# Turning attention's output in 32x32 blocks on VectorE instead of by products on TensorE and transposing transfers

## What is computed

```python
qkv = x @ w_qkv                                   # 16 heads, q, k, v of 16 columns each
scores = einsum('...hqd,...hkd->...hqk', q, k) / sqrt(256)
attn = softmax(where(causal, scores, -1e30))
out = einsum('...hqk,...hkd->...qhd', attn, v).reshape(..., 256)
return out @ w_o
...
h = layernorm(x) * (1 + ca) + sa
x = x + ga * attention(h)
h = layernorm(x) * (1 + cb) + sb
x = x + gb * ffn(h)                               # shared silu(h w1) * (h w2) w3 + the two chosen experts
```

## Time and profile before

| | us |
|---|---|
| median of 3 runs | 1907.32 (1906.16 to 1908.15) |
| the profiled execution, its own time | 1906.43 |
| its span | 1904.7 |
| TensorE busy | 1759.5 (92%) |
| VectorE busy | 1506.3 (79%) |
| ScalarE busy | 1126.2 (59%) |
| GpSimd busy | 955.2 (50%) |

### The profile page before, as it was taken

How to read it: one execution, slowest core, us unless ns; L and a number is a source line. 1 busy time by engine, 2 the same in 40 slices (tenths; PEclk the granted TensorE clock), 3 DMA queues, 4 the chain that set the end, 5 groups by cost and what they waited for, 6 DMA issues and landing times. The chain is left out here.

```text
span 1904.7 us, 46834 instructions
## 1 busy us (share of the span) xinstructions
PE 1759.5 (92%) x17886; PEld 1014.6 (53%) x17886; DVE 1506.3 (79%) x2717; ACT 1126.2 (59%) x1486; POOL 955.2 (50%) x1015
## 2 busy tenths in 40 slices
PE   5677899999999999999999999999999999989987
PEld 2233435455554454445454545454545788778764
DVE  7886788887988787788878888988896486755777
ACT  2687867676767576767666766776676333222211
POOL 2444555365436553654454554545555267534423
PEclk8788999999999999999999999999999999999989
DMA  4243331223122312231122122221312777766997
GB/s 144 74 150 84 119 70 44 68 58 97 24 74 55 96 32 66 56 96 41 58 58 85 44 60 54 83 63 47 85 52 83 167 159 165 176 142 145 276 315 260
DMA packets 248840, 191.58 MB, mean 101 GB/s; under 512 B 181344, under 2 KB 216936, under 8 KB 246832
## 3 DMA queue, kind: packets, MB, share of 16 engines
q1 hardware_dynamic: 235472, 152.26, 32.1%
q0 software_dynamic: 12960, 36.06, 5.5%
q10 hardware_dynamic: 192, 0.26, 0.1%
HBM read 65.23 MB, written 62.19 MB: 67 GB/s over the span
## 5 line engine op out<-in xcount | busy, mean ns | idle before, releaser
L1176 ACT ACTIVATE arena<-pair 128x1024 f32<-128x1024 f32 (+1 forms) x640 | 575.5, 942 | 195.3 <-PE pair L1898 192.4
L1370 DVE TENSOR_REDUCE max_part<-pair 128x2 f32<-128x1024 f32 (+2 forms) x448 | 535.0, 1219 | 95.6 <-PE pair L1874 91.7
L1935 PE MATMUL pair<-feat_parts,ffn_sb 128*128 128x512 f16 x1536 | 379.0, 383 | 9.9 <-DMA feat_parts<-rows 5.4
L1920 PE MATMUL pair<-arena,v_sb 128*32 128x256 f32 (+1 forms) x5120 | 325.1, 367 | 2.0 <-ACT arena L1176 1.0
L950 POOL TENSOR_SCALAR_AFFINE_SELECT arena<-arena 128x512 f32<-128x512 f32 x256 | 169.5, 670 | 290.7 <-ACT arena L1176 290.4
L1874 PE MATMUL pair<-arena 48*128 48x128 f16 (+3 forms) x2304 | 209.9, 280 | 40.7 <-DMA arena<-parts 13.5
L1898 PE MATMUL pair<-arena 50*128 50x256 f16 (+1 forms) x2560 | 210.4, 264 | 22.6 <-DVE max_part L1370 7.9
L1935 PEld LDWEIGHTS pair<-feat_parts,ffn_sb 128*128 128x128 f16 x1536 | 132.7, 98 | 179.5 <-issue 38.6
L1959 PE MATMUL pair<-parts,arena 128*128 128x256 f16 x1704 | 209.6, 282 | 18.5 <-DMA parts<-lists 10.0
L1036 POOL DMA_INDIRECT slots<-arena,feat x142 | 145.0, 1021 | 145.9 <-DVE arena L1599 116.0
L1042 POOL TENSOR_TENSOR hidden<-silu_h,hidden 128x512 f16<-128x512 f32 x128 | 151.4, 1187 | 121.0 <-ACT hidden L1211 120.0
(11 more groups left out here) (221 smaller groups left out, 2251.5 us busy)
## 6 DMA issues: line engine op xcount, KB each, us to landing
arena<-parts SPq DMA_DIRECT2D x380, 64.0 KB, 2.3
rows<-x SPq DMA_DIRECT2D x8, 1024.0 KB, 5.4
x_sb<-x SPq DMA_DIRECT2D x16, 512.0 KB, 4.8
base<-norm SPq DMA_DIRECT2D x14, 512.0 KB, 3.2
ffn_parts<-hidden SPq DMA_DIRECT2D x8, 768.0 KB, 4.1
arena<-ffn_parts SPq DMA_DIRECT2D x8, 768.0 KB
x_sb<-ffn_w SPq DMA_DIRECT2D x6, 768.0 KB, 5.8
norm<-ffn_w SPq DMA_DIRECT2D x6, 768.0 KB, 5.6
```

The source lines that it names most:

```text
L1176: sc.activation(to[:, :, lo:QC], of[:, :, lo:QC], ACT.Exp, scale=SCALE / QK_SCALE ** 2).then_inc(exp_done, 1)
L1370: return vec.tensor_reduce(to, of, AX.X, ALU.max)
L1920: last = mm(to[32 * j:32 * j + 32, lo:QC], v_sb[:, kt, h:h + 32], probs[:, u % RING, at + lo:at + QC], start=(kt == 0), stop=(kt == 2 * c ...
L1935: last = mm(to[:, 0:512], w_up[s][W_PART[i]][:, f, m * RH + h * P:m * RH + (h + 1) * P], feat_parts[:, A_PART[i], f, c * 512:(c + 1) * 512 ...
```

## The change

The accumulator is turned on VectorE, in blocks of 32x32: VectorE's transpose reads it in PSUM and writes `o_raw` in SBUF, where partition 32j + r then holds queries r, r + 32, ... of head j with 32 columns each, 16 values, the sum and 15 unused ones. `raw` is now that step, on VectorE in place of ScalarE. `turn_out`, its products and its bank are gone. `normalise` reads `o_raw`, and writes `o_tok` in a new arrangement (`o_blocks`) in which heads stay on their partitions. When the four groups of a block of queries are there, `osp` turns that block of 128x512 in place on VectorE, again in 32x32 blocks; the result has features on partitions. ScalarE and GpSimd then write the two float16 parts into `o_feat` directly. The transposing DMAs of L721 are gone. The features stand in a permuted order, so `w_o` is loaded in the same order, in eight DMAs, issued after the other first loads. The waits follow: `raw` waits for `values_done` on VectorE's queue, ScalarE's part of `osp` for `o_turned`, and for the earlier use of `feat`; the output product waits for `o_low` in place of the DMAs.

```diff
-            def turn_o(f, c):
-                sp.wait_ge(o_low, f * O_SPLIT + c + 1)
...
-                for t in range(2 * c, 2 * c + 2):
-                    sp.dma_start_transpose(o_feat[:, :, :, t * P:(t + 1) * P].rearrange("p a f n -> p (a f) n"),
-                                           rows16[:, t, 0:2 * D]).then_inc(o_in[c // 2], 16)
...
-            for dst, src in ((wv_in, w_v), (wo_in, w_o), (rw_in, router_w), (bias_sb[:, :], bias)):
+            for dst, src in ((wv_in, w_v), (rw_in, router_w), (bias_sb[:, :], bias)):
...
+            for j in range(GH):
+                for a in range(2):
+                    to, of = 32 * j + HD * a, GH * HD * a + HD * j
+                    sp.dma_start(wo_in[to:to + HD, :, :], w_o[of:of + HD, :, :]).then_inc(wo_landed, 16)
...
-                t = slice(2 * c, 2 * c + 2)
-                gp.tensor_tensor(rows16[:, t, D:2 * D], o_tok[:, t, :], rows16[:, t, 0:D], ALU.subtract).then_inc(o_low, 1)
+                of = o_blocks[:, c, :].rearrange("p (f n) -> p f n", f=NF)
+                t = slice(c * QC, (c + 1) * QC)
+                gp.tensor_tensor(o_feat[:, 1, :, t], of, o_feat[:, 0, :, t], ALU.subtract).then_inc(o_low, 1)
...
-            def raw_copy(b, n):
-                act.wait_ge(values_done, at_unit(b, end_of(n)))
-                if past(at_step(b, n - 2)):
-
-                    act.wait_ge(out_turned, at_step(b, n - 2))
-                sc.activation(o_raw[:, n % 2, :], gathered(b, n), ACT.Copy).then_inc(raw_ready, 1)
...
-                        act.wait_ge(o_ready, at_step(f, STEPS - NQ + c))
-                        act.wait_ge(head_turned, at_half(min(b, B - 1), 1))
+                        act.wait_ge(o_turned, f * O_SPLIT + c + 1)
+                        act.wait_ge(feat1_low, at_half(min(f + 1, B - 1), 1))
                         if past(f):
-                            act.wait_ge(listed_done, at_half(f - 1, 1) * LISTED)
-                        sc.activation(rows16[:, 2 * c:2 * c + 2, 0:D], o_tok[:, 2 * c:2 * c + 2, :], ACT.Copy).then_inc(o_high, 1)
+                            act.wait_ge(op_full, at_half(f - 1, 1))
+                        sc.activation(o_feat[:, 0, :, c * QC:(c + 1) * QC], o_blocks[:, c, :].rearrange("p (f n) -> p f n", f=NF), ACT.Copy).then_inc(o_high, 1)
...
-            def normalise(b, v, n, base):
+            def turn_raw(b, n):
+                if past(at_step(b, n - 2)):
+                    dve.wait_ge(o_ready, at_step(b, n - 2))
+                dve.wait_ge(values_done, at_unit(b, end_of(n)))
+                vec.transpose(o_raw[:, n % 2, :], gathered(b, n)).then_inc(raw_ready, 1)
+
+            def normalise(b, n, base):
                 g, c = n % STEPS // NQ, n % NQ
-                dve.wait_ge(out_turned, at_step(b, n))
-                o = buffer_of(v, ("to", n))[:, 0:QC].rearrange("p (k n) -> p k n", k=2 * GH)
+                dve.wait_ge(raw_ready, at_step(b, n))
+                o = o_raw[:, n % 2, :].rearrange("p (q r) -> p q r", r=32)
                 chain(vec.reciprocal(l_inv[:, n % 2, :], o[:, :, HD]), base)
...
+                to = o_blocks[:, c, QC * (g // 2):QC * (g // 2 + 1)].rearrange("p (q a d) -> p q a d", a=2, d=HD)[:, :, g % 2, :]
+                vec.tensor_tensor(to, o[:, :, 0:HD], l_inv[:, n % 2, :].unsqueeze(2).to_broadcast([P, 2 * GH, HD]), ALU.mult).then_inc(o_ready, 1)
+
+            def turn_o(f, c):
+                dve.wait_ge(o_ready, at_step(f, STEPS - NQ + c))
+                vec.transpose(o_blocks[:, c, :], o_blocks[:, c, :]).then_inc(o_turned, 1)
...
-            def turn_out(b, v, n):
-                pe.wait_ge(raw_ready, at_step(b, n))
-                to = take(b, v, ("to", n))
-                for t in range(QC // P):
-                    last = nc.tensor.transpose(to[:, t * P:(t + 1) * P], o_raw[:, n % 2, t * P:(t + 1) * P], ident[:, :])
-                last.then_inc(out_turned, 1)
...
-                        pe.wait_ge(o_in[h], (f + 1) * TURNED)
+                        pe.wait_ge(o_low, f * O_SPLIT + 2 * h + 2)
```

More of the change, by code:

```diff
@@ L158 @@
+        scores:72 max:0:15 max:0:16 values:68 raw:13 share:11 max:0:17 diag_max:0:14 values:69 values:70 values:71
+        scores:73 scores:74 raw:14 scores:75 values:72 values:73 scores:76 normalise:13 shifts:0 normalise:14
+        scores:77 values:74 values:75 scores:78 scores:79 max_turn:0
     """,
     "second": """
-        max:1:0 osp:0 max:1:1 select_max:1:1 max:1:2 values:-4 max:1:3 values:-3 osp:1 max:1:4 max:1:5
-        scores:0 values:-2 values:-1 diag_max:1:1 raw:-1 max:1:6 scores:1 scores:2 scores:3 max:1:7 max:1:8 select_max:1:5 values:0 values:1 raw:0
@@ new lines @@
+        scores:20 scores:21 down:-1:0 max:2:3 max:2:4 values:18 values:19 raw:3 values:20 router:0
+        scores:22 scores:23 down:-1:1 route:0 up:0:0 up:0:1 up:0:2 up:0:3 down:-1:2 store:-1 rank:0 place:0 scatter:0 scatter:1 up:0:4 up:0:5 values:21 raw:4
+        values:22 scores:24 scores:25 normalise:3 up:1:0 up:1:1 scores:26 diag_max:2:1 max:2:5 max:2:6 max:2:7 select_max:2:5 scatter:2 scatter:3 values:23
+        scatter:4 up:1:2 scores:27 up:1:3 up:1:4 up:1:5 hid:0 scores:28 hid:1 max:2:8 diag_max:2:5 values:24 values:25 scatter:5 scatter:6 scatter:7 max:2:9
@@ new lines @@
+        scores:4 scores:5 scores:6 raw:0 osp:1 osp:2 max:1:11 max:1:12 up:-1:0 up:-1:1 up:-1:2 hid:-2 values:2
+        scores:7 up:-1:3 up:-1:4 up:-1:5 hid:-1 max:1:13 diag_max:1:10 max:1:14 osp:3 values:3 normalise:0 values:4 values:5
+        scores:8 op:0 scores:9 raw:1 scores:10 values:6 values:7 rest:0 values:8 max:1:15 scores:11 max:1:16 down:-4:0 max:1:17 select_max:1:14
+        scores:12 values:9 values:10 values:11 scores:13 scores:14 scores:15 diag_max:1:14 shifts:1 var:0 down:-4:1 down:-4:2 count:0 lengths:0 normalise:1
@@ new lines @@
+        scores:51 scores:52 down:1:0 down:1:1 diag_max:3:10 halves:1 max:3:15 select_max:3:14 max:3:16 values:50 values:51 raw:10 down:1:2 down:2:0
+        scores:53 scores:54 max:3:17 down:2:1 down:2:2 scores:55 values:52 diag_max:3:14 values:53 values:54
+        scores:56 ln:1 scores:57 scores:58 shifts:3 max_turn:3 table_rest:0:0 values:55 router:1 down:3:0 route:1 fetch:0 fetch:1 up:8:0 up:8:1 up:8:2 up:8:3
+        up:8:4 up:8:5 up:9:0 up:9:1 down:3:1 down:3:2 load_x:0 up:9:2 up:9:3 up:9:4 hid:8 up:9:5 scores:59
```

365 lines of the change are left out of this document (167 added, 198 removed).

## The result

The changed kernel takes 1919.6 us (median of 7 runs, 1911.5 to 1928.1) against 1907.3 us for the kernel before, run beside it; the ratio is 1.0069, 95% interval 1.0041 to 1.0097. Run again beside other kernels it was 1.0071 (1.0042 to 1.0101). The forecast was 1877 us, with a range of 1850 to 1908. So the prediction was wrong in sign: it missed by 43 us, and the time lies 12 us over the range.

The account below looks back on a forecast made before the run. TensorE was taken to set the time from 196 to 1495 us, seven batches. Terms -39 - 1 + 13 - 3 = -30 us gave a span of 1875 us, and 1877 us as the time; range 1850 to 1908.

Parts of the forecast that it names:

- TensorE loses the transposes: 256 transposes leave TensorE, 0.35 us a step: 39 us (35 to 44) off in the seven TensorE-bound batches.
- VectorE gains the block transposes: 128 PSUM transposes at 0.421 us and 32 in SBUF at 0.733 add 77 us to VectorE, 9.7 a batch.
- Rival (3): VectorE's block transpose takes each float32 element in two passes: 127 us, about 1906 us, no change; chance 0.06.
- What VectorE's load costs: Less idle VectorE makes TensorE's weight loads wait longer for row maxima: 1.8 us a batch, 13 in seven (0 to 45).
- the order: New order of row maxima, scores and FFN products in all batches: not priced, widens the range some 8 us either way.
- The first batch: TensorE has 41 us of slack from 48 to 196 us, so removing its transposes there gains 1 us (0 to 5).
- the end: Start of the last stage: without transposing transfers on SP's queue, TensorE waits less for experts' weights; 3 us off (0 to 6).
- Rival (2): VectorE's in-order queue becomes the bound; batch 187.4 us if idle shrinks only to 24: 1931 us, slower; chance 0.15.
- Rival (1): Waits are free and TensorE's share comes back whole: batch of 177.5 us, kernel 1855 us; chance 0.20.
- (4): Raw transposes wait for values at the head of VectorE's queue, 4 us a batch in place of 1.8: 1892 us; chance 0.09.

Follow-up runs that it names:

- one-input kernel: Changed kernel with the normalisation's product replaced by a one-input reduction over one element, division by the softmax sum left out; 1875.6 us, 0.9866 of the kernel before.
- The kernel with two moves: Changed kernel with two normalisations of the repeated batch moved in VectorE's order, at its head and step 14; 0.9914, 1884.4 us; 0.9772 on another, slower chip.

## Why the prediction was wrong

*The step that failed.* "The reciprocal (200 ns) and the product of the normalisation keep their element counts and read SBUF where they read PSUM; nothing is counted for that." For the reciprocal, with one input, that held (191 ns, against 200). For the product the new place of its operand was the whole matter: 31.5 us of holds on VectorE, 18.8 of them in the five at the head of a batch (4 x 4.3 + 3.0, less 5 x 0.29). By the ratios they cost 1.0069 - 0.9866 = 0.020, or 39 us, against a forecast gain of 30. The miss is 43 us.

*It could have been read from the trace of before.* The prediction asked for the mean of each shape, not for its spread. VectorE's subtraction in the last stage, whose two inputs are both in SBUF, has a median of 685 ns and a longest of 1645; 3 of its 48 take over 1 us, each beside GpSimd's subtraction of L1042:

```profile
L1592 DVE TENSOR_TENSOR arena<-arena x48: 679/685/1645, 1506.7 to 1863.8; 128x512 f16<-128x512 f32 x48
```

```profile
1813.83 1.23 DVE L1616 TENSOR_TENSOR feat<-feat,wqk_sb 128x1024 f32<-128x1024 f32 x1
1814.97 1.65 DVE L1592 TENSOR_TENSOR arena<-arena 128x512 f16<-128x512 f32 x1
```

```profile
1814.21 1.86 POOL L1042 TENSOR_TENSOR hidden<-silu_h,hidden 128x512 f16<-128x512 f32 x1 [2.83 <-ACT hidden L1211]
```

The one at 1814.97 began while GpSimd's subtraction ran, which ended at 1816.07, and it ended 0.55 us after that. In the earlier trace rows the same group stands with its mean of 733 ns, used as a price, which hid this. And the product of before, with one input in PSUM, was 290/291/293 beside the same GpSimd.

*TensorE loses the transposes.* Right. With one input TensorE is busy 1719.6 us (1712 forecast) and a repeated batch takes 180.1 us (the mean of the last four; 179 to 180 forecast), with 6.3 us of idle in 184 (7 forecast). In the changed kernel that gain is given back: 1741.2 us of busy time, with 256 products fewer than before. The likely reason is the clock, 0.956 of full over its span against 0.971 with one input: its products at 1.2 GHz take longer.

*VectorE gains the block transposes.* Right: 439 and 691 ns (0.421 and 0.733 taken), 77.8 us in all against 77. Rival (3) is out. VectorE's 1589.5 us agrees with the 1583 forecast only by chance. With one input it is 1560.7, and the changed kernel has the holds on top. The lengths of VectorE's instructions added one by one are 1697.7 us with one input and 1622.3 before, so 75 us more, as forecast; but instructions back to back overlap a little in the profile (row maxima start at 768.41 above, before the product ends at 768.49), busy time counts that once, and there is more of it now. So added lengths are not added busy time: VectorE was to be 91% busy in a repeated batch, and is 88% with one input.

*What VectorE's load costs,* 13 us, and *the order,* 8 us either way: together right to 5 us, by the one-input kernel; apart they weren't measured. That the cost depends on where VectorE's instructions stand is seen by moving all normalisations, which cost 43 us with no product held (1.0091 against 0.9866), a part of it perhaps through the bank that TensorE gets back later.

*The first batch* (1 us) and *the end* (3 us) are not tested by the table's outer parts, -3.6 and -2.3 us in the changed kernel, since both hold stretches of the batches that TensorE bounds. From the end of the last product of `values` to the end of the span it takes 409.4 us in place of 414.7: 5 less, within the 0 to 6 of the forecast. For the first batch alone nothing was measured.

*The rivals.* Rival (2) has the right sign and nearly its signature: TensorE at 94.1% in 184 us (it asked for under 94), VectorE idle 23.6 us, TensorE's longest wait (3.9 us) for row maxima. Its mechanism is not the one. VectorE's idle time is much the same with one input (20.9 us in 184), where the batch is 9 us shorter. What lengthened the batch was no lack of slack in VectorE on average but a single hold of 4 us at a place without any. Rival (1) is out, since even with one input a batch takes 180.1 us and not 177.5; so is the wait of (4), since the raw transposes wait for `values` 9.9 us in the whole span, not 4 us a batch.

*What stays open.* The kernel with two moves still lies 0.005 over the one-input kernel, with 9.4 us of holds left, mostly between 210 and 390 us; whether those explain it wasn't tried. Which of GpSimd's instructions hold the product is seen in part: in the changed kernel masks and subtractions stand beside held ones, while none of the 8 products that start beside its small L948 (`rstd`) is held, and of the 16 that start beside an indirect DMA (L1008) 11 are not. Why one product gets in between two GpSimd instructions and another doesn't is open. The price of the clock after a hold was not separated from that of the wait by a run of its own.

## What to carry to other kernels

When an operand moves from PSUM to SBUF, look at what else the instruction reads: with a second input in SBUF, a VectorE instruction can wait for a whole row of GpSimd instructions that run back to back beside it, here up to 4.3 us for 0.29 us of work. Read the least, median and longest of such a group, in the trace of before too, not its mean. And price a hold by the place: 4.1 us in front of row maxima that TensorE needed cost 7.5 us with the clock, while the gain from moving five of 1.5 us with idle time behind them could not be told from the noise. So moving one instruction in the order turned a loss of 0.7% into a gain of 0.8%.

## What the runs showed of the hardware

- The held product did not get in when the first GpSimd instruction ended, but after five of them in a row, at 768.34 us; it ended 0.15 us later. That is not always so: the product at 308.40 us ended 0.14 us after one GpSimd instruction, though the next followed at once. GpSimd's own keep their lengths beside a waiting product (1.10 us beside a held product, 1.11 beside a one-input reduction). In the last stage of the kernel before, the GpSimd subtraction that began during VectorE's two-input product of L1616 took 1.86 us, against a median of 1.16; so GpSimd may be held as well, by an instruction that came first, which no run tests.
- The block transpose of float32 takes 439 ns for 128x256 from PSUM to SBUF, 455 ns from PSUM into the same bank, and 691 ns for 128x512 in place in SBUF; none is held by GpSimd.
- One idle stretch of 3.9 us on TensorE is followed by up to 20 us in which the granted clock is partly at its lower level (0.67 and 0.84 in two stretches of 10 us), worth 4.9 us of full speed; where the same stretch was made by a reduction, 6.1 us, against 1.7 us at that place of the batch without it. So the clock costs about as much as the idle time.
